# A decoder layer on one core: first batch's x^T in row-tile order, its 1/std in one pass, and a new order of the instructions

## Chip, cores and metric

The kernel runs on 1 core of a Trainium2 chip. The metric is device microseconds of one execution, lower is better. The kernel before takes 381.44 us (median of 3 runs, 380.48 to 382.34).

## The reference

Eight batches of 512 tokens with 256 features go through one decoder layer, all in float32:

```python
x = x + attn(layernorm(x), head_mask, w_q, w_k, w_v, w_o)   # one head of 128; softmax(q k^T / sqrt(128)) v
x = x + xattn(layernorm(x), ctx, mask, W, b)                # relu(x W^T + b) against relu(ctx W^T + b), masked softmax, times ctx
x = x + ffn(layernorm(x), w_gate, w_up, w_down)             # 256 -> 1024 -> 256, silu(gate) * up
```

In the ffn the activations are rounded to whole multiples of max|row|/127, and the weights to -1, 0 or 1 times the mean of |w|. Layer normalisation is (x - mean) / sqrt(var + 1e-5) over the features.

## The kernel before, in words

There are three streams per batch. Stream A is self-attention, B is cross-attention, C is the ffn. E prepares the context side of B (YP0 and YP1, relu(ctx W^T + b) by halves), W and F load and prepare the weights. Everything is written out by hand in five tables, one for each engine (`PE_ORDER`, `ACT_ORDER`, `DVE_ORDER`, `POOL_ORDER`, `SP_ORDER`). An entry such as `A.S0/3` is stream, step and batch, and each engine runs its table in order, with semaphore waits in front of each step. The three streams of different batches run through each other: A is one to two batches ahead of B, and B one ahead of C. The tables alone decide what stands behind what.

To keep float32 accuracy, each operand of a matmul in A, B and E is split into hi (rounded to fp32r, on ACT) and lo (the rest, on DVE or POOL), and a product is three matmuls (hi hi, hi lo, lo hi; L1047 to L1049). A 512-wide block is one PSUM bank. PE therefore carries most of the work. ACT copies PSUM to the hi part and does exp, relu, tanh and silu. DVE makes lo parts, row maxima, statistics (`bn_stats`, `bn_aggr`) and residual additions. POOL makes other lo parts (L617 to L630), 1/std (an addition and a power), gate times up (L674) and rounding. SP issues DMAs.

A takes the layer norm out of the matmul: the weights are centred, q, k and v are computed from the raw x^T (`a_xT_raw`, 2 chunks of 128 features by 512 tokens), and 1/std of each token is applied later: to the scores as a row vector over the keys (`r_bc`, 128 x 512, the same row on all partitions) and as a per-partition factor over the queries, and to v^T (`vT`, L1444).

Partition p of a tile of x holds tokens 4p to 4p+3 (own_tokens), so 1/std of a batch is a 128 x 4 tile `a_rstd`, and its columns are in the order (t p) where x^T has token order (p t). For batches 1 to 7 `r_bc` comes by a DMA through DRAM (`r_rows`). For batch 0 it is made on the core: `a_rstd` (128 x 4) is split into `r0_hi` (ACT, L814) and `r0_lo` (DVE, L1316), each is spread over a diagonal with `ident` (`spread_r0`, L1321, into `hT_hi` and `hT_lo`), and PE multiplies by ones (step W.r, L1269 and L1271, bank b0), so that each partition gets the row. ACT copies it to `r_bc` and turns (t p) into (p t) in its output pattern (`set_r0`, L818). q of any batch is written back from (p t) to (t p) by the copy that makes q_hi (L795) and q_lo (L1415), so that 128 consecutive columns are one tile of queries. The trace leaves digits out of names: `r_hi` and `r_lo` are `r0_hi` and `r0_lo`.

The first steps are: loads of the first context, of w_qkv, W and x; column sums of w_qkv on PE (L1262) and centring on DVE (`centre`, L1551, two instructions); YP0 and YP1 of batch 0; the split of w_qkv (ACT L980, then DVE `W.split`, L1556), which Q of batch 0 waits for; Q, K, V; W.r; then VT (transposes of v^T, L1082), the scores S0 to S3, exp, the transposes P0 to P3 (L1093), H and Y. YP1 of batch 0 uses bank b0, so W.r must wait until ACT has read it (L859, L860), and each relu on ACT waits for POOL to have taken the lo part of the one before (L625).

## Time and profile before

| | |
|---|---|
| median of 3 runs | 381.44 us (380.48 to 382.34) |
| the profiled execution, its own time | 382.19 us |
| its span | 380.2 us |
| TensorE busy (PE) | 364.1 us, 96% |
| DVE, ACT, POOL busy | 319.8 (84%), 320.0 (84%), 294.2 us (77%) |
| DMA | 36.92 MB, mean 97 GB/s |

The span is what the profiler saw between the first and the last instruction, and the execution's own time holds 2.0 us more around it. Busy time of PE counts an overlap of matmuls that follow each other, since one matmul is reported with a duration of 0.39 us although the next starts 0.23 us after it.

### The profile page before, as it was taken

The page shows a single profiled execution, that of the slowest core. Times are in us where ns is not written, and L with a number is a line of the kernel's source. Part 1 is how long each engine was busy: PE and PEld are TensorE (multiplying, and loading weights), DVE is VectorE, ACT ScalarE, POOL GpSimd, SP SyncE. Part 2 cuts the span into 40 slices and gives each one's busy share as a digit, 9 for nine tenths or more (in the row PEclk, how much of TensorE's full clock was granted, in tenths as well). Part 3 has the DMA queues.
Part 4 walks back from the last instruction along what each step waited for, and adds up shares of the span by engine and source line. Part 5 has one row for each costly group of instructions (what it writes and reads, how often), then busy time and mean ns, then how long its engine had stood idle before and what let it go on. Part 6 is the DMA issues. An engine that isn't in the chain of part 4 may idle for free.

```text
span 380.2 us, 7393 instructions
## 1 busy us (share of the span) xinstructions
PE 364.1 (96%) x2113; PEld 284.7 (75%) x2142; DVE 319.8 (84%) x921; ACT 320.0 (84%) x598; POOL 294.2 (77%) x425
## 2 busy tenths in 40 slices
...
PEclk9989999999999999999999999999999999999999
...
DMA packets 48167, 36.92 MB, mean 97 GB/s; under 512 B 39552, under 2 KB 41216, under 8 KB 47744
## 3 DMA queue, kind: packets, MB, share of 16 engines
...
## 4 chain that ended last, share of the span: by engine, by line
PE 79%; ACT 7%; DVE 5%; DMA 4%; issue 3%; POOL 1%; ACTq 0%; DVEq 0%; POOLq 0%; SPq 0%
PE b_bank L1047 9%; PE b_bank L1049 9%; PE b_bank L1048 9%; PE d_bank L1251 7%; PE a_bank L1047 6%; PE a_bank L1049 6%; PE a_bank L1048 6%; PE g_bank L1235 5%; PE u_bank L1235 5%; PE b_bank L1163 3%; PE a_bank L1093 3%; DMA a_xT_raw<-in_x_t 2%; PE e_bank L1047 1%; PE e_bank L1049 1%; PE e_bank L1048 1%
## 5 line engine op out<-in xcount | busy, mean ns | idle before, releaser
L674 POOL TENSOR_TENSOR c_work<-c_work 128x512 f32<-128x512 f32 x48 | 61.8, 1290 | 18.1 <-DVE c_work L1491 16.1
L716 POOL TENSOR_SCALAR c_work<-c_work,h_q 128x1024 f32<-128x1024 f32 x31 | 34.9, 1125 | 11.5 <-DVE h_q L1511 11.5
L1504 DVE TENSOR_REDUCE h_max<-c_work 128x1 f32<-128x1024 f32 x32 | 38.8, 1213 | 4.2 <-POOL c_work L674 3.6
L935 ACT ACTIVATE c_work<-g_bank,c_tanh_scale 128x512 f32<-128x512 f32 x52 | 36.0, 692 | 6.4 <-PE g_bank L1235 4.9
L1047 PE MATMUL b_bank<-ctx_hi,b_pT_hi 128*128 128x256 f32 x128 | 38.6, 302 | 0.0
L1491 DVE SCALAR_TENSOR_TENSOR c_work<-c_work,g_bank 128x512 f32<-128x512 f32 x52 | 35.3, 679 | 2.1 <-ACT c_work L935 1.8
L1049 PE MATMUL b_bank<-ctx_hi,b_pT_lo 128*128 128x256 f32 x128 | 36.1, 282 | 0.0
L1048 PE MATMUL b_bank<-ctx_lo,b_pT_hi 128*128 128x256 f32 x128 | 36.1, 282 | 0.0
L1251 PE MATMUL d_bank<-downT,c_half 128*128 128x256 bf16 x256 | 33.3, 273 | 1.5 <-ACT a_xT_raw L962 0.9
L945 ACT ACTIVATE c_half<-c_work 128x1024 bf16<-128x1024 f32 x28 | 29.7, 1066 | 4.1 <-POOL c_work L716 4.1
L1235 PE MATMUL g_bank<-gateT,xqT 128*128 128x512 bf16 x98 | 30.5, 381 | 1.5 <-ACT xqT L908 0.5
L1251 PEld LDWEIGHTS d_bank<-downT,c_half 128*128 128x128 bf16 x256 | 23.9, 98 | 10.3 <-issue 3.0
L1235 PE MATMUL u_bank<-upT,xqT 128*128 128x512 bf16 x97 | 30.3, 381 | 1.0
L938 ACT ACTIVATE c_work<-u_bank 128x512 f32<-128x512 f32 x48 | 29.0, 603 | 1.8 <-PE u_bank L1235 1.5
L625 POOL TENSOR_TENSOR yp_lo<-e_relu,yp_hi 128x512 fp32r<-128x512 f32 x16 | 20.7, 1293 | 9.7 <-ACT yp_hi L860 9.7
L1047 PE MATMUL b_bank<-yp_hi,xp_hi 128*128 128x512 f32 x64 | 28.0, 437 | 0.0
L847 ACT ACTIVATE b_pT_hi<-b_bank 128x512 fp32r<-128x512 f32 x32 | 19.2, 599 | 9.4 <-PE b_bank L1163 9.4
L1047 PEld LDWEIGHTS b_bank<-ctx_hi,b_pT_hi 128*128 128x128 f32 x128 | 24.3, 190 | 2.4 <-issue 0.7
L838 ACT ACTIVATE a_p<-a_p,a_nmax 128x512 f32<-128x512 f32 x32 | 23.5, 733 | 2.7 <-DVE a_nmax L1437 2.7
L869 ACT ACTIVATE b_p<-b_p,b_nmax 128x512 f32<-128x512 f32 x32 | 23.3, 731 | 2.3 <-DVE b_nmax L1469 2.3
L1049 PE MATMUL b_bank<-yp_hi,xp_lo 128*128 128x512 f32 x64 | 25.2, 393 | 0.0
L1048 PE MATMUL b_bank<-yp_lo,xp_hi 128*128 128x512 f32 x64 | 25.1, 392 | 0.0
...
## 6 DMA issues: line engine op xcount, KB each, us to landing
...
c_work<-in_w_up SPq DMA_DIRECT2D x1, 1024.0 KB, 10.2
```

The costliest lines, as they stand in the source:

```text
L674: pool.tensor_tensor(h[:, t % 2, half * HALF:(half + 1) * HALF], th[:, j % 2, :], up[:, j % 2, :], ALU.mult).then_inc(hs, 1)
L716: pool.tensor_scalar(h[:, t % 2, :], h[:, t % 2, :], h_q[:, t:t + 1], ROUND if n < LAST else ROUND_F16, ALU.mult, ALU.add).then_inc(h_roun ...
L935: act.activation(th[:, j % 2, :], gu_bank("g", j, n), ACT.Tanh, scale=c_tanh_scale[:, j // 2:j // 2 + 1]).then_inc(tanhs, 1)
L938: act.activation(up[:, j % 2, :], gu_bank("u", j, n), ACT.Copy).then_inc(ups, 1)
L945: act.activation(h_q8[:, t % 2, :], h[:, t % 2, :], ACT.Copy, bias=-ROUND).then_inc(hqs, 1)
L1047: pe.matmul(dst, l_hi, r_hi, start=first, stop=False)
L1048: pe.matmul(dst, l_hi, r_lo, start=False, stop=False)
L1049: return pe.matmul(dst, l_lo, r_hi, start=False, stop=last)
L1235: mm = pe.matmul(dst, xqT[:, t * DC + c, :], w[:, c, cols], start=c == 0, stop=c == DC - 1)
L1251: mm = pe.matmul(d_bank[:, 0:D], h_T[:, t % 2, f, :], downT[:, f, :], start=f == 0, stop=f == FC - 1)
L1491: dve.scalar_tensor_tensor(th[:, j % 2, :], th[:, j % 2, :], 1.0, gu_bank("g", j, n), ALU.add, ALU.mult).then_inc(gates, 1)
L1504: dve.tensor_reduce(h_max[:, one], h[:, t % 2, :], AX.X, ALU.max, apply_absolute_value=True).then_inc(h_maxes, 1)
```

## The change

1. The host lays x^T of batch 0 out as (t p), in row-tile order; batches 1 to 7 stay as they were. So `set_r0` copies the bank to `r_bc` straight, and q_hi and q_lo of batch 0 are straight copies too.
2. 1/std of batch 0 is one addition and one power over 128 x 4 (`a_rstd_first`) in place of two of each over 128 x 2. It starts when both halves of the statistics are there.
3. `r0_lo` is made by four instructions of one column each (tensor_scalar with the hi column as its scalar) in place of one over 128 x 4.
4. All five order tables are new. Among others: SP loads W ahead of the second half of the first context, and x of batch 1 ahead of the second half of x of batch 0; PE runs W.r ahead of V.

```diff
@@ PE_ORDER (one line of it shown)
-    W.colsum/0 E.YP0/0 E.YP1/0 A.Q/0 A.K/0 A.V/0 W.r/0 A.VT/0 A.S0/0 A.S1/0 A.S2/0 A.S3/0 A.P0/0 A.P1/0 A.Q/1
+    W.colsum/0 E.YP0/0 E.YP1/0 A.Q/0 A.K/0 W.r/0 A.V/0 A.VT/0 A.S0/0 A.S1/0 A.S2/0 A.S3/0 A.P0/0 A.P1/0 A.Q/1
...
@@ POOL_ORDER
-    A.rs0/0 A.rs1/0 E.YP0/0 A.rs0/1 A.rs1/1 E.YP1/0 A.xT0/1 A.xT1/1 E.ctxT/1 A.rs0/2 A.rs1/2 B.ctx/0 E.YP0/1
+    A.rs0/0 E.YP0/0 E.YP1/0 A.rs0/1 A.rs1/1 A.xT0/1 A.xT1/1 A.rs0/2 A.rs1/2 E.ctxT/1 A.xT0/2 A.xT1/2 B.ctx/0
...
@@ SP_ORDER
-    W.c0/0 W.qkv/0 W.c1/0 W.W/0 W.x0/0 W.x1/0 S.x/1 W.bias/0 W.o/0 W.hm/0 F.gate/0 F.up/0 F.down/0 S.ctx/0
+    W.c0/0 W.qkv/0 W.W/0 W.c1/0 W.x0/0 S.x/1 W.x1/0 W.bias/0 W.o/0 W.hm/0 F.gate/0 F.up/0 F.down/0 S.mask/0
...
+            def a_rstd_first():
+                pool.wait_ge(a_mvs, 2)
+                pool.tensor_tensor(a_var[:, :], a_mv[:, :, 1], eps[:, :], ALU.add).then_inc(a_rstds, 2)
+                pool.wait_ge(a_rstds, 2)
+                pool.tensor_tensor(a_rstd[:, 0, :], a_var[:, :], neg_half[:, :], ALU.pow).then_inc(a_rstds, 2)
             def a_rstd_part(half, n):
                 two = slice(2 * half, 2 * half + 2)
                 pool.wait_ge(a_mvs, 2 * n + half + 1)
-                if n > 0:
-                    pool.wait_ge(a_rstds, 4 * (n - 1) + 2 * half + 2)
+                pool.wait_ge(a_rstds, 4 if n == 1 else 4 * (n - 1) + 2 * half + 2)
...
-                    a_rstd_part(int(name[2]), n)
+                    a_rstd_part(int(name[2]), n) if n > 0 else a_rstd_first()
...
+                elif step == "Q" and n == 0:
+                    act.activation(q_hi[:, :], src[:, :], ACT.Copy, scale=SCALE).then_inc(a_his, 1)
...
             def set_r0():
                 act.wait_ge(r0_filled, 1)
-                act.activation(r_bc[:, :].rearrange("k (p t) -> k t p", t=T), b0_bank[:, :].rearrange("k (t p) -> k t p", t=T),
-                               ACT.Copy).then_inc(r0_set, 1)
+                act.activation(r_bc[:, :], b0_bank[:, :], ACT.Copy).then_inc(r0_set, 1)
...
             def split_r0_rest():
                 dve.wait_ge(r0_his, 1)
-                dve.tensor_tensor(r0_lo[:, :], a_rstd[:, 0, :], f32(r0_hi[:, :]), ALU.subtract).then_inc(r0_los, 1)
+                for t in range(T):
+                    last = dve.tensor_scalar(r0_lo[:, t:t + 1], a_rstd[:, 0, t:t + 1], f32(r0_hi[:, t:t + 1]), None, ALU.subtract)
+                last.then_inc(r0_los, 1)
...
-                    if step == "Q":
+                    if step == "Q" and n == 0:
+                        last = dve.scalar_tensor_tensor(q_lo[:, :], src[:, :], SCALE, f32(q_hi[:, :]), ALU.mult, ALU.subtract)
+                    elif step == "Q":
...
     x, ctx = inputs["x"], inputs["ctx_1024"]
+    x_t = x.reshape(*x.shape[:2], -1, P).transpose(3, 0, 2, 1).copy()
+    x_t[:, 0] = x_t[:, 0].reshape(P, x_t.shape[2], P, -1).swapaxes(2, 3).reshape(P, *x_t.shape[2:])
```

What the tables do is seen in the instructions of an engine in their order (line numbers are those of each kernel; code lines of the new one stand up to 12 further on).

DVE at the start, from the last split of the first inputs to the spread of 1/std. Before:

```order
L1326 TENSOR_TENSOR ctxT_lo<-ctxT_raw,ctxT_hi 128x512
L1568 TENSOR_TENSOR wt_lo<-xqT,wt_hi 128x512
L1551 SCALAR_TENSOR_TENSOR b_p<-b_bank,b_p 128x384 x2
L1304 BN_STATS a_bn<-x_all 128x6 x4
L1311 BN_AGGR a_mv<-a_bn 128x2 x2
L1556 TENSOR_TENSOR wqkv_lo<-b_p,wqkv_hi 128x768
L1311 BN_AGGR a_mv<-a_bn 128x2 x2
L1304 BN_STATS a_bn<-x_all 128x6 x4
L1311 BN_AGGR a_mv<-a_bn 128x2 x4
L1316 TENSOR_TENSOR r_lo<-a_rstd,r_hi 128x4
```

DVE in the changed kernel, the same place:

```order
L1334 TENSOR_TENSOR ctxT_lo<-ctxT_raw,ctxT_hi 128x512
L1310 BN_STATS a_bn<-x_all 128x6 x2
L1561 SCALAR_TENSOR_TENSOR b_p<-b_bank,b_p 128x384 x2
L1310 BN_STATS a_bn<-x_all 128x6 x2
L1317 BN_AGGR a_mv<-a_bn 128x2 x2
L1571 CAST hm_f<-hm_i 128x1
L1317 BN_AGGR a_mv<-a_bn 128x2 x2
L1310 BN_STATS a_bn<-x_all 128x6 x2
L1566 TENSOR_TENSOR wqkv_lo<-b_p,wqkv_hi 128x768
L1310 BN_STATS a_bn<-x_all 128x6 x2
L1574 SCALAR_TENSOR_TENSOR wo_lo<-b_p,hm_f,wo_hi 128x256
L1323 TENSOR_SCALAR r_lo<-a_rstd,r_hi 128x1 x4
```

`ctxT_lo` and `wt_lo` are the second context half and W; `b_p` is the centring of w_qkv and `wqkv_lo` its split, which Q waits for. The statistics of batch 0 (two of four `BN_STATS`) now come ahead of the centring, and two of batch 1's ahead of `wqkv_lo`; the scaling of w_o (`hm_f`, `wo_lo`), which stood behind `q_lo`, now comes ahead of `r_lo`.

ACT at the start, from YP0 of batch 0 to the copies of 1/std and k. Before:

```order
L859 ACTIVATE e_relu<-e_bank,bias 128x512
L860 ACTIVATE yp_hi<-e_bank,bias 128x512
L814 ACTIVATE r_hi<-a_rstd 128x4
L795 ACTIVATE q_hi<-a_bank 128x512
L830 ACTIVATE gateT,w_sum<-c_work 128x1024
L859 ACTIVATE e_relu<-b_bank,bias 128x512
L860 ACTIVATE yp_hi<-b_bank,bias 128x512
L830 ACTIVATE gateT,w_sum<-c_work 128x1024
L818 ACTIVATE r_bc<-b_bank 128x4x128
L798 ACTIVATE k_hi<-a_bank 128x512
```

ACT in the changed kernel, the same place:

```order
L865 ACTIVATE e_relu<-e_bank,bias 128x512
L866 ACTIVATE yp_hi<-e_bank,bias 128x512
L830 ACTIVATE wo_hi<-b_p,hm_f 128x256
L821 ACTIVATE r_hi<-a_rstd 128x4
L865 ACTIVATE e_relu<-b_bank,bias 128x512
L866 ACTIVATE yp_hi<-b_bank,bias 128x512
L799 ACTIVATE q_hi<-a_bank 128x512
L836 ACTIVATE gateT,w_sum<-c_work 128x1024
L805 ACTIVATE k_hi<-a_bank 128x512
L825 ACTIVATE r_bc<-b_bank 128x512
```

`e_bank` is YP0 and `b_bank` under L859/L865 is YP1; `gateT,w_sum` is a sum over half of an ffn weight. YP1 moved ahead of `q_hi` and of the first sum, `k_hi` ahead of `r_bc`, and the second sum behind both.

ACT near the end, from the last copy of B's output (`a_xT_raw<-b_bank`, O3 of batch 7) to the third rounded row tile of the ffn of batch 6 (`c_half`). Before:

```order
L953 ACTIVATE a_xT_raw<-b_bank,b_inv 128x256
L935 ACTIVATE c_work<-g_bank,c_tanh_scale 128x512
L908 ACTIVATE xqT<-e_bank 128x256
L935 ACTIVATE c_work<-a_bank,c_tanh_scale 128x512
L962 ACTIVATE a_xT_raw<-d_bank,h_out 128x256
L902 ACTIVATE c_xn<-c_xn,pos_round,c_q 128x256
L897 ACTIVATE c_xn<-x_all,c_shift,c_rstd 128x256
L923 ACT_TABLE_LOAD
L923 ACTIVATE c_work<-g_bank,c_tanh_scale 128x512
L908 ACTIVATE xqT<-e_bank 128x256
L945 ACTIVATE c_half<-c_work 128x1024
```

ACT in the changed kernel, between the same two ends:

```order
L959 ACTIVATE a_xT_raw<-b_bank,b_inv 128x256
L903 ACTIVATE c_xn<-x_all,c_shift,c_rstd 128x256
L929 ACT_TABLE_LOAD
L929 ACTIVATE c_work<-g_bank,c_tanh_scale 128x512
L903 ACTIVATE c_xn<-x_all,c_shift,c_rstd 128x256
L929 ACTIVATE c_work<-a_bank,c_tanh_scale 128x512
L908 ACTIVATE c_xn<-c_xn,pos_round,c_q 128x256
L951 ACTIVATE c_half<-c_work 128x1024
```

`ACT_TABLE_LOAD` and `c_work<-g_bank` under L923/L929 is the first silu of batch 7. Eleven rows became eight: two tanh of batch 6 (L935), two copies of `xqT` and one of the ffn output (L962) are no longer between the two ends, and a second silu and a second norm (L897/L903) are.

## Rows read from the trace of the kernel before

**Rows 1.** The page: TensorE's busy time, and its granted clock in 40 slices.
```profile
PE 364.1 (96%) x2113; PEld 284.7 (75%) x2142; DVE 319.8 (84%) x921; ACT 320.0 (84%) x598; POOL 294.2 (77%) x425
...
PEclk9989999999999999999999999999999999999999
```

**Rows 2.** Windows by stage: busy us of PE, PEld, DVE, ACT, POOL, PEclk, DMA, GB/s.
```profile
19.00:27.00 8.00, 5.96 (x23) 4.50 (x24) 5.50 (x16) 7.06 (x15) 3.35 (x3) 0.79 0.75 258
27.00:57.00 30.00, 28.23 (x153) 23.22 (x152) 23.40 (x82) 28.64 (x53) 24.72 (x22) 1.00 0.40 118
57.00:354.00 297.00, 294.71 (x1734) 232.55 (x1760) 258.79 (x750) 253.14 (x479) 240.21 (x344) 1.00 0.31 77
354.00:372.70 18.70, 15.90 (x113) 9.25 (x114) 17.69 (x42) 17.86 (x33) 15.52 (x34) 1.00 0.22 44
```

**Rows 3.** Timeline of the first 23 us: start us, us taken, engine, line, instruction.
```profile
9.52 1.02 DVE L1551 SCALAR_TENSOR_TENSOR b_p<-b_bank,b_p 128x384 f32<-128x384 f32 x2
...
9.66 0.50 PE L1047 MATMUL e_bank<-ctxT_hi,wt_hi 128*128 128x512 f32 x1 [0.44 <-DVE wt_lo L1568]
...
10.46 1.40 DVE L1304 BATCH_NORM_STATS2 a_bn<-x_all 128x6 f32<-128x256 f32 x4
...
11.91 0.93 DVE L1556 TENSOR_TENSOR wqkv_lo<-b_p,wqkv_hi 128x768 fp32r<-128x768 f32 x1
...
12.90 0.51 PE L1047 MATMUL a_bank<-a_xT_hi,wqkv_hi 128*128 128x512 f32 x1 [0.19 <-DVE wqkv_lo L1556]
...
13.92 0.70 POOL L653 TENSOR_TENSOR a_rstd<-a_var,neg_half 128x2 f32<-128x2 f32 x1
...
14.59 1.29 POOL L625 TENSOR_TENSOR yp_lo<-e_relu,yp_hi 128x512 fp32r<-128x512 f32 x1
...
14.89 1.00 DVE L1316 TENSOR_TENSOR r_lo<-a_rstd,r_hi 128x4 fp32r<-128x4 f32 x1
...
17.42 1.06 ACT L830 ACTIVATE gateT<-c_work 128x1024 f32<-128x1024 f32 x1
...
17.64 0.47 PE L1269 MATMUL b_bank<-hT_hi,ones_r 128*128 128x512 f32 x1 [0.38 <-issue]
...
18.46 1.09 ACT L818 ACTIVATE r_bc<-b_bank 128x512 f32<-128x512 f32 x1
...
19.32 0.65 ACT L798 ACTIVATE k_hi<-a_bank 128x512 fp32r<-128x512 f32 x1
...
20.40 0.66 PE L1082 MATMUL u_bank<-ident,vT 128*128 128x128 f32 x4 [2.05 <-DVE vT L1444]
...
22.49 0.63 PE L1048 MATMUL a_bank<-k_lo,q_hi 128*128 128x512 f32 x1
...
22.91 0.63 PE L1049 MATMUL a_bank<-k_hi,q_lo 128*128 128x512 f32 x1
```

**Rows 4.** Timeline of PE: the first matmuls of Q of batch 1.
```profile
27.06 0.47 PE L1047 MATMUL d_bank<-a_xT_hi,wqkv_hi 128*128 128x512 f32 x1
27.37 0.39 PE L1048 MATMUL d_bank<-a_xT_lo,wqkv_hi 128*128 128x512 f32 x1
27.60 0.40 PE L1049 MATMUL d_bank<-a_xT_hi,wqkv_lo 128*128 128x512 f32 x1
```

**Rows 5.** Windows of the start: the granted clock from 22 to 24 us.
```profile
22.00:24.00 2.00, 2.00 (x6) 1.55 (x5) 1.18 (x3) 1.96 (x5) 0.48 (x1) 0.50 0.96 376
```

**Rows 6.** Timeline of PE from 41 to 55 us: the two waits.
```profile
47.87 0.47 PE L1047 MATMUL e_bank<-ctxT_hi,wt_hi 128*128 128x512 f32 x1 [0.92 <-ACT yp_hi L860]
...
53.77 0.36 PE L1047 MATMUL a_bank<-wo_hi,hT_hi 128*128 128x256 f32 x1 [0.63 <-DVE hT_lo L1423]
```

**Rows 7.** Timeline of ACT near the end: O3 of batch 7, third tile of batch 6.
```profile
354.82 0.46 ACT L953 ACTIVATE a_xT_raw<-b_bank,b_inv 128x256 f32<-128x256 f32 x1
...
360.23 1.06 ACT L945 ACTIVATE c_half<-c_work 128x1024 bf16<-128x1024 f32 x1
```

**Rows 8.** Timeline of DVE near the end: first gate product of batch 7.
```profile
361.42 0.69 DVE L1486 TENSOR_TENSOR c_work<-c_work,u_bank 128x512 f32<-128x512 f32 x1 [0.16 <-ACT c_half L945]
```

280 lines of the change are left out of this document (140 added, 140 removed).

## The prediction

> **What bounds the kernel now.** I read four views, in this order. First the page: TensorE is busy 364.1 of 380.2 us, no other engine is over 84%, and its granted clock is full but for one dip in the third slice [rows 1]. Then the windows by stage, for where PE's idle time lies [rows 2]: 2.0 us from 19 to 27, 1.8 us from 27 to 57, only 2.3 us in the 297 us from 57 to 354, and 2.8 us from 354 to 372.7. In the long middle PE is the bound. All its matmuls are still there after the change, and so a new order of them can give back idle time, and nothing else: at most 1.8 + 2.3 = 4.1 us between 27 and 354, however good it is. Its two largest pieces are single waits of 0.92 us on ACT's relu (YP of the context side) and 0.63 us on DVE's lo part of h [rows 6]. The third view is the timeline of the first 27 us, where PE waits for other engines [rows 3, 4], and the last is the timeline near the end, where ACT and DVE pace the last ffn [rows 7, 8]. A microsecond gained before Q of batch 1 at 27.06 us is worth about one at the end, since PE runs nearly without a gap from there. I ask three things: when does Q of batch 1 start, does the middle keep its idle time, and does the tail get shorter.
>
> **The start now.** YP begins at 9.66 us and Q at 12.90, as soon as `wqkv_lo` (11.91 to 12.84) is there. 1/std is ready at 14.62 (13.92 + 0.70). The one-row product starts at 17.64, the copy to `r_bc` takes 1.09 us from 18.46, and the transposes of v^T start at 20.40 after 2.05 us of idle PE [rows 3]. By 22 us the clock is at half, 1.2 of its 2.4 GHz (0.50 from 22 to 24 us [rows 5]): two score matmuls stand 0.42 us apart (22.49, 22.91 [rows 3]) where they stand 0.23 apart at full clock (27.37, 27.60 [rows 4]). The mean clock of 0.79 over the 8 us from 19 to 27 [rows 2] bounds the cost of the dip: 8 x 0.21 = 1.7 us of PE work.
>
> **The parts of the change.**
>
> *Straight copy to r_bc.* It took 1.09 us [rows 3]. The nearest copy of 128x512 out of PSUM without a reordered pattern is `k_hi`, 0.65 us [rows 3]. Gain 0.44 us, on the path to VT. Straight copies of q gain between 0 and 0.44; no row has q straight, and I take 0: they're hidden, since K and v^T are what the scores wait for.
>
> *1/std in one pass.* Two operations in place of four on POOL. The power over two columns took 0.70 us; over four I bound it by 0.70 and 1.40 and take 1.0, in the middle. For the addition in front of it I allow 0.2, a guess. The new pair starts when both halves of the statistics are there, about 12.4 (below), and ends at 13.6 where the old ended at 14.62: 1.0 us sooner. I cost it at nothing, because 1/std is not late: the row product also needs YP1's relus (its bank), the lo part and the spreads. If those cover it no more, it is worth 1.0.
>
> *r_lo by columns.* The old one took 1.00 us for four elements a partition, from 14.89 to 15.89, and POOL's `yp_lo` ran from 14.59 to 15.88: it stood behind POOL [rows 3]. Four single columns cost from 4 x 0.07 to 1.29 us (the same stand behind POOL); I take 0.3. Gain 0.7, hidden by ACT, see below.
>
> *The new DVE order.* W comes before the second context half now, so one DVE instruction of 0.6 to 0.7 us (a 128x512 one took 0.69 [rows 8]) is no longer ahead of `wt_lo`: YP begins at 9.0, and its twelve matmuls of 0.23 end at 11.8. But half of the statistics (0.70 of 1.40 us [rows 3]) now stands ahead of the centring, and half of batch 1's (0.70) ahead of `wqkv_lo`. Counting on from 9.5: statistics to 10.2, centring to 11.15, the other statistics to 11.85, 0.45 for aggregates and a small cast to 12.3 (a guess), statistics of batch 1 to 13.0. So `wqkv_lo` starts 1.1 us later than now. There it meets POOL's power (12.6 to 13.6), and as `r_lo` shows, such a pair does not run together. I let it wait until 13.6. It ends at 14.4, and **Q starts at 14.4 in place of 12.90**, with PE idle 2.6 us from 11.8.
>
> *The new ACT order.* YP0's relus end at 13.2, the copies of w_o and r_hi at 13.9; YP1's relus must wait for POOL's lo part of YP0, which itself stands behind `wqkv_lo`: 14.4 to 15.7. So YP1 ends at 16.9, q_hi at 17.5, one ffn sum (1.06 us and 0.2 to read it out [rows 3]) at 18.7, k_hi at 19.3, r_bc at 19.9. The spreads on DVE, behind POOL's two lo parts, are ready between 17.2 and 18.9, so they are covered. v^T follows at 20.5, and VT starts at 20.6 in place of 20.40. The straight copy's 0.44 us and the rest are spent on the later split and on YP1, sum and k ahead of it.
>
> *The clock.* An idle PE of 2.05 us is followed by the half clock now; the new idle stretch of 2.6 us lies earlier, before Q and K. I expect the dip there, over the twelve matmuls of Q and K: K's copy and then V come later, VT at 21.6, but the scores run at full clock and end at about 25.0 (now 25.4). Counting exp and transposes behind them, Q of batch 1 starts at 27.1: no change. With the dip on the scores as now it is 27.3 (+0.2); without any dip 26.3 (-0.8). The Trainium skill, TensorE: Matmul & The Clock Gate, section "Why this matters for your kernels", lets the clock fall only for pauses longer than the 2.05 us seen here. The trace speaks against that: it fell. By the rule the start would come out at -0.8.
>
> **Start: 0.0 us** (from -0.8 to +1.5, the upper end below).
>
> *The middle.* Loads and stores move, and so do the lanes of all streams. **0.0 us**: the bound below is -4.1 (all idle time gone), the bound above I set at the same +4.1, and I take the zero between, since I see no reason why a new order should make more waits vanish than appear; the two single waits stay, since what stands ahead of them on ACT is exchanged for work of the same length (a sum or sign of 1.0 us against two relus).
>
> *The tail.* Between the copy of O3 (354.82) and the third rounded tile of batch 6 (360.23), ACT passes 5.4 us; that tile releases the first gate product of batch 7 at 361.42, which starts the row of products and maxima that DVE runs to the end [rows 7, 8]. Now eight operations and a table load stand between, then five and a table load: less by two tanh, two small copies and one of 128x256 out of PSUM, and more by a silu and a norm. Taking the load as 1.3 us, the copy and eight operations share 4.1 us, 0.46 each, and three of them are 1.4 us. Against it, O3 on PE comes behind four more gate and up steps (two matmuls of 0.23 each, 1.8 in sum) and no longer behind one down step (eight of half that width, 0.9): 0.9 us later. **-0.5 us**, between -1.4 (O3's lateness costs nothing) and +0.9 (ACT was not the limit).
>
> **Sum:** 0.0 + 0.0 - 0.5 = -0.5 us on the profiled execution's own 382.19 us, 381.7. That execution stands 0.75 us above the median of the three, so on the median: 381.44 - 0.5 = **380.9 us**.
>
> **The rivals.**
>
> *A, faster: the dip is gone and the order packs better.* The row product is ahead of V now, so V's 1.4 us of matmuls fill what was an idle PE; with PE fed, the clock stays up. Start -0.8, tail -0.5, and half of the 4.1 us of idle middle won, -2.0: 381.44 - 3.3 = 378.1. For it: the idle time is real, and the straight copy is on the path. Against: an idle stretch of 2.6 us arises before Q. The skill's rule on the clock, above, belongs here. Chance 0.33.
>
> *B, slower: `wqkv_lo` loses its turn to POOL.* If POOL takes `yp_lo` (1.29 us) straight after the power, `wqkv_lo` runs from 14.9 and Q starts at 15.7. Everything of batch 0 is then late by up to 1.3 us, and the clock dips on Q and again after the wait before VT. It decides once POOL gets the turn: +1.5 at the start, and +1.0 in the middle, where A's later batches then meet B's work, with the tail at -0.5: 381.44 + 2.0 = 383.4. For it: `r_lo` waited for the whole of a `yp_lo`. Against: DVE asks first here. Chance 0.22. Nearby, the middle alone could be 2 us worse.
>
> *C: the change does nothing at the start, and the tail neither,* because 1/std was not late and O3's lateness eats ACT's gain: 381.4, inside the forecast's band. Chance 0.12.
>
> My forecast has the remaining 0.33.
>
> **The numbers.** A measurement of this kernel can tell about 0.5%, 1.9 us. Faster than 379.5: most of A and a little of the forecast, 0.34. Slower than 383.3: half of B, 0.11, and 0.09 from the forecast and C where the middle comes out 2 us worse. Within: 0.46. The range goes from A, with 0.5 us more of the middle, 377.6, to B with 0.4 more, 383.8.
>
> **What would show each step.** Right: the row of `r_bc` takes 0.6 to 0.65 us; `r_lo` takes 0.1 to 0.2 for one column; `a_rstd` of batch 0 is one row of about 1.0 us before 14 us; YP begins near 9.0 and Q after 14.0, with over 2 us of idle PE between; the clock falls before 18 us; Q of batch 1 starts at 26.5 to 27.5; PE idles 3 to 5 us from 27 to 354; the first silu's gate product stands under 6.1 us behind the copy of O3 (now 6.6). Wrong: Q before 13.5 (DVE's order costs nothing), Q of batch 1 before 26 or after 28, or PE's idle time in the middle below 2 or above 6 us, which would move the time more than all of the start.

## The result and the profile after

The changed kernel takes **385.22 us** (median of 5 runs, 384.90 to 386.25) beside 381.44 us before (5 runs, 380.48 to 382.77): ratio 1.0099, 95% interval 1.0082 to 1.0116. It is 1% slower, 3.8 us, and outside the range of the prediction. The profiled execution took 384.94 us, with a span of 383.0 in place of 380.2.

The windows by stage (busy us of PE, PEld, DVE, ACT, POOL, then PEclk, DMA, GB/s), after:

```profile
19.00:27.00 8.00, 5.34 (x25) 4.24 (x26) 5.86 (x23) 7.41 (x18) 3.39 (x5) 0.89 0.92 298
27.00:57.00 30.00, 28.15 (x149) 23.28 (x148) 21.12 (x70) 26.74 (x48) 24.25 (x21) 0.97 0.42 117
57.00:354.00 297.00, 293.47 (x1719) 231.94 (x1743) 256.68 (x747) 255.27 (x478) 239.31 (x340) 1.00 0.34 75
354.00:372.70 18.70, 16.48 (x104) 10.04 (x106) 16.58 (x40) 16.43 (x30) 14.95 (x36) 0.91 0.30 72
```

Against [rows 2]: PE leaves 3.5 of the 297 us from 57 to 354 idle (297.00 - 293.47), where it left 2.3. Both figures are too high by much the same: these two traces hold 2115 and 2113 matmuls for 2142 weight loads, and in this stretch 24 and 26 matmuls have no row (before's lacks gate and up matmuls, 195 rows for 224). What they took counts as idle time. The profiles with all 2142 and the old order behind the start leave 0.3 to 0.6 us idle there (e1, e3 and e14 below). Its clock is 0.89 from 19 to 27 us (0.79 before), but 0.97 behind that and 0.91 in the tail, where it was full.

The timeline of the first 28 us, after (start us, us taken, engine, line, instruction, idle time before it and what ended it):

```profile
8.48 0.50 PE L1053 MATMUL e_bank<-ctxT_hi,wt_hi 128*128 128x512 f32 x1 [0.66 <-DVE wt_lo L1578]
...
12.21 1.03 POOL L646 TENSOR_TENSOR a_rstd<-a_var,neg_half 128x4 f32<-128x4 f32 x1
12.27 0.94 DVE L1566 TENSOR_TENSOR wqkv_lo<-b_p,wqkv_hi 128x768 fp32r<-128x768 f32 x1
...
13.27 0.50 PE L1053 MATMUL a_bank<-a_xT_hi,wqkv_hi 128*128 128x512 f32 x1 [1.74 <-DVE wqkv_lo L1566]
...
17.75 0.61 ACT L825 ACTIVATE r_bc<-b_bank 128x512 f32<-128x512 f32 x1
...
19.26 0.66 PE L1088 MATMUL u_bank<-ident,vT 128*128 128x128 f32 x4 [0.86 <-DVE vT L1454]
...
19.67 0.48 PE L1053 MATMUL d_bank<-k_hi,q_hi 128*128 128x512 f32 x1
...
19.91 0.63 ACT L882 ACTIVATE mask_add<-mask_u 128x512 f32<-128x512 uint8 x1 [0.50 <-DMA mask_u<-in_mask]
...
21.48 0.58 ACT L805 ACTIVATE v_hi<-u_bank 128x512 fp32r<-128x512 f32 x1
...
23.00 0.62 ACT L813 ACTIVATE a_xT_hi<-a_xT_raw 128x512 fp32r<-128x512 f32 x1
...
23.52 0.71 ACT L844 ACTIVATE a_p<-a_p,a_nmax 128x512 f32<-128x512 f32 x1
23.69 2.51 POOL L617 TENSOR_TENSOR a_xT_lo<-a_xT_raw,a_xT_hi 128x512 fp32r<-128x512 f32 x2 [4.20 <-ACT a_xT_hi L813]
...
24.23 0.61 ACT L813 ACTIVATE a_xT_hi<-a_xT_raw 128x512 fp32r<-128x512 f32 x1
...
24.47 0.63 PE L1099 MATMUL g_bank<-ident,a_p 128*128 128x128 f32 x4 [1.80 <-ACT a_p L844]
...
26.43 0.78 PE L1053 MATMUL d_bank<-a_xT_hi,wqkv_hi 128*128 128x512 f32 x1
```

The first score matmul and the first exp of before, for comparison:

```profile
21.00 0.50 PE L1047 MATMUL d_bank<-k_hi,q_hi 128*128 128x512 f32 x1
...
24.44 0.72 ACT L838 ACTIVATE a_p<-a_p,a_nmax 128x512 f32<-128x512 f32 x1 [0.48 <-DVE a_nmax L1437]
```

This answers to [rows 3]. YP starts at 8.48 (9.66 before), Q at 13.27 (12.90), the copy to r_bc takes 0.61 us (1.09) and stands at 17.75 (18.46), VT at 19.26 (20.40), and the first scores at 19.67 (21.00), 1.3 us sooner and at full clock. So far the change does more than I forecast. Then it is given back. ScalarE (ACT) waits 0.50 us for the first mask's load, and a sum, v_hi and another sum follow, then x^T of batch 1 at 23.00 and the first exp at 23.52: 0.9 us sooner than before (24.44), of the 1.3. PE has stood idle for 1.80 us when the first exp's transposes begin. The other half of x^T stands behind that exp, at 24.23, POOL's lo parts of both halves end at 26.20 (23.69 + 2.51), and Q of batch 1 starts at 26.43: 0.6 us sooner [rows 4]. And it starts at half clock: its first matmul takes 0.78 us, where that of Q took 0.50.

In the middle, the waits of PE from 57 to 354 us (waiter, releaser: us in total, times, longest us), in before and after:

```profile
PE a_bank L1093 <- ACT a_p L838: 0.3, 1, 0.3
```

```profile
PE d_bank L1257 <- DMA c_half<-c_half: 0.6, 1, 0.6
PE a_bank L1088 <- DVE vT L1454: 0.4, 2, 0.2
PE g_bank L1241 <- issue: 0.2, 1, 0.2
PE g_bank L1241 <- DVE c_work L1501: 0.2, 1, 0.2
PE b_bank L1053 <- POOL xp_lo L630: 0.2, 1, 0.2
```

Before has one such wait, and that is all the view lists: 0.3 us. After, the waits come to 1.6 us, and the largest is PE's wait for a transposing DMA of the ffn's activations, which ends at 120.80 us, ahead of the first down step of batch 0. The tail, after, in the timeline of ACT and DVE, and the window of 2 us in which its clock is lowest:

```profile
357.09 0.47 ACT L959 ACTIVATE a_xT_raw<-b_bank,b_inv 128x256 f32<-128x256 f32 x1 [1.00 <-PE b_bank L1055]
...
361.50 1.05 ACT L951 ACTIVATE c_half<-c_work 128x1024 bf16<-128x1024 f32 x1
...
362.68 0.69 DVE L1496 TENSOR_TENSOR c_work<-c_work,u_bank 128x512 f32<-128x512 f32 x1 [0.73 <-ACT c_half L951]
...
363.10 0.53 PE L1241 MATMUL g_bank<-gateT,xqT 128*128 128x512 bf16 x1 [1.16 <-ACT xqT L914]
```

```profile
364.00:366.00 2.00, 2.00 (x10) 0.96 (x8) 1.90 (x3) 1.79 (x4) 1.03 (x4) 0.50 0.63 118
```

The first gate product of batch 7 stands 5.6 us behind the copy of O3 (357.09 to 362.68), where it stood 6.6 us behind [rows 7, 8]. But PE then idles 1.16 us ahead of a gate step at 363.10, and its clock is at 0.50 from 364 to 366 us.

### The profile page after: what moved, and what is told of

Read it like the earlier page. It is cut to its first block, busy times and chain, and to the rows that moved or that the text cites. A ratio compares the mean times of both kernels' runs of the same rounds, so it can differ in the third digit from the quotient of the medians.

```text
span 383.0 us, 7397 instructions
## 1 busy us (share of the span) xinstructions
PE 364.0 (95%) x2115; PEld 285.2 (74%) x2142; DVE 318.4 (83%) x924; ACT 322.2 (84%) x598; POOL 293.0 (76%) x423
## 4 chain that ended last, share of the span: by engine, by line
PE 60%; POOL 14%; ACT 7%; DMA 6%; issue 6%; DVE 4%; SPq 2%; ACTq 0%; POOLq 0%; DVEq 0%
PE b_bank L1053 7%; PE b_bank L1055 7%; PE b_bank L1054 7%; PE d_bank L1257 5%; PE a_bank L1053 4%; PE g_bank L1241 4%; PE a_bank L1055 4%; PE a_bank L1054 4%; POOL c_work L679 4%; PE u_bank L1241 4%; DMA mask_u<-in_mask 3%; PE b_bank L1169 3%; PE a_bank L1099 2%; POOL xp_lo L630 1%; PE a_bank L1241 1%
## 5 line engine op out<-in xcount | busy, mean ns | idle before, releaser
L1241 PE MATMUL u_bank<-upT,xqT 128*128 128x512 bf16 x100 | 31.4, 386 | 0.8
L617 POOL TENSOR_TENSOR a_xT_lo<-a_xT_raw,a_xT_hi 128x512 fp32r<-128x512 f32 x14 | 17.9, 1287 | 9.8 <-ACT a_xT_hi L813 9.8
L1054 PEld LDWEIGHTS b_bank<-ctx_lo,b_pT_hi 128*128 128x128 f32 x128 | 24.4, 191 | 0.4
```

The lines of the kernel that those rows point to most:

```text
L1054: pe.matmul(dst, l_hi, r_lo, start=False, stop=False)
L1241: mm = pe.matmul(dst, xqT[:, t * DC + c, :], w[:, c, cols], start=c == 0, stop=c == DC - 1)
```

## The experiments

The theory to begin with: the order costs the time, and most of it behind the start, where the profiled pair shows PE's idle time grow. Its rivals: the edits cost it, or the start does. Before stands at 381.3 to 382.1 us in the five sets of runs, so ratios to it are what to compare. A ratio of 0.0026 is 1 us.

**The edits or the order?** Two kernels: the local edits in the order of before, and the new order with the instructions of before.

```diff
 e1: every ORDER table as before, the rest as in the change
-    A.rs0/0 A.rs1/0 E.YP0/0 A.rs0/1 A.rs1/1 E.YP1/0
+    A.rs0/0 E.YP0/0 A.rs0/1 A.rs1/1 E.YP1/0
 e2: the new tables, the rest as before
-    A.rs0/0 E.YP0/0 E.YP1/0 A.rs0/1 A.rs1/1
+    A.rs0/0 A.rs1/0 E.YP0/0 E.YP1/0 A.rs0/1 A.rs1/1
```

> The local edits alone (row-tile order of x^T of batch 0, straight copies, 1/std in one pass, lo part by columns), with the five order tables of before. Theory (the new order costs the time, the edits save a little): 380.9 to 381.5, that is 0 to 0.5 us below before, the copy to r_bc 0.61 us in place of 1.09, and scores 0.4 us sooner. Rival (the edits cost: the addition and the power wait for both halves of the statistics, or four column instructions stand behind POOL): 382 to 384, with the one-row product later than the 17.6 us of before.

> The new order tables alone, with the instructions of before (reordering copy to r_bc, 1/std in two passes, lo part in one). Theory (order costs the time): 385 to 386, about as slow as the change or 0.5 us slower. Rival (edits cost): 381 to 383.

Measured: e1 381.79 us, ratio 1.0005 (0.9990 to 1.0020); e2 385.06 us, 1.0086 (1.0064 to 1.0108). The order costs the time, as the theory has it, and the edits give nothing that can be told (0.4 us less to 0.8 more). In e1's profile the path to the scores is shorter all the same:

```profile
17.97 0.59 ACT L820 ACTIVATE r_bc<-b_bank 128x512 f32<-128x512 f32 x1
...
20.02 0.50 PE L1048 MATMUL d_bank<-k_hi,q_hi 128*128 128x512 f32 x1
...
25.27 0.47 PE L1048 MATMUL d_bank<-a_xT_hi,wqkv_hi 128*128 128x512 f32 x1
```

The copy takes 0.59 us, the first score stands 1.0 us sooner than before, and Q of batch 1 at 25.27 in place of 27.06, with a clock of 1.00 in every window up to 372.7 us. But this was the fastest of twelve executions (380.37), and the median shows nothing of those 1.8 us. Of before's 23 executions in this set, 14 have a mean granted clock of at least 0.998, with a median of 381.0, and 9 a lower one, with 381.8. The dip is worth 0.8 us, and it comes and goes.

**Which part of the order?** The tables are cut where both orders have issued the same steps: PE behind B.XP0/0, ACT behind B.norm1/0, DVE behind A.Y1/1, POOL behind B.rs1/0, SP behind S.rb/1. PE comes to its cut some 53 to 57 us into the program, and SP, whose queue runs ahead, at some 36 us.

```diff
 e3: the change, and in every table behind the cut the order of before, PE:
     A.Y0/1 A.Y1/1 B.XP0/0
-    A.Q/2 B.XP1/0 A.K/2 E.YP0/3 A.V/2 B.S0/0
+    B.XP1/0 A.Q/2 A.K/2 E.YP0/3 A.V/2 B.S0/0
 e4: the reverse, before the cut the order of before, PE:
-    A.K/0 W.r/0 A.V/0 A.VT/0
+    A.K/0 A.V/0 W.r/0 A.VT/0
```

> The change's instructions; the new order up to B.XP0 of batch 0 on TensorE (and the same place on the other engines), the order of before behind it. Theory 1 (the loss sits where the profiled pair shows it grow: start +0.2, middle +1.5, tail +1.0): 381.2 to 382.0, no slower than before. Rival (the later start of the sums, mask and exps in the first batch, and the half clock that moves to 25 to 29 us, set off the rest): 383.5 to 385.

> The change's instructions; the order of before up to B.XP0 of batch 0, the new order behind it. Theory 1 (the loss sits in the middle and the tail): 383.5 to 385, 2.5 to 3.5 us above before. Rival (the loss comes from the start): 380.5 to 382.

Measured: e3 383.22 us, 1.0037 (1.0020 to 1.0053); e4 388.77 us, 1.0176 (1.0149 to 1.0203). e3 lies between both theories: the new start costs 1.2 us against e1 by the ratios (1.4 by the medians) even with the old rest, though the two intervals just touch, so my reading of the profiled pair, +0.2, was wrong. e4 has a wait of its own at the cut:

```profile
35.21 0.67 ACT L874 ACTIVATE mask_add<-mask_u 128x512 f32<-128x512 uint8 x1
...
35.95 0.33 SPq L514 DMA_DIRECT2D mask_u<-in_mask  x1
...
36.37 0.38 SPq L486 DMA_DIRECT2D a_xT_raw<-in_x_t  x1
...
41.28 0.63 ACT L805 ACTIVATE a_xT_hi<-a_xT_raw 128x512 fp32r<-128x512 f32 x1 [4.70 <-DMA a_xT_raw<-in_x_t]
```

SP's queue runs in order too. The new order loads the third mask ahead of x^T of batch 2, and has the first mask's conversion (mask_add), which frees the buffer, early on ACT. With the old start that conversion ends at 35.88, the mask's load starts at 35.95, x^T behind it at 36.37, and ACT stands for 4.70 us. e5 mends only this:

```diff
 e5: as e4, SP_ORDER
-    S.rb/1 S.mask/2 S.xT/2 S.rw/2 S.ctxT/2 S.xT/3 S.ctx/1
+    S.rb/1 S.xT/2 S.ctxT/2 S.rw/2 S.mask/2 S.ctx/1 S.xT/3
```

> As the kernel with the new order behind the first 53 us only, but SP's queue keeps the order of before for ten entries more, so that x^T of batch 2 is issued ahead of the third mask. Theory (the 5 us stall at 38 us in the first version was the third mask's load standing in front of x^T of batch 2, and the rest of the new order costs 2 us, as the change against the kernel with the new start alone: 385.2 against 383.2): 383.5 to 384.5. Rival (the new rest needs the new start and costs more behind the old one): 386 to 388.

Measured: 382.58 us, 1.0011 (0.9998 to 1.0023). Below the range of the theory: the new rest costs 0.2 us against e1 here, and e5 is at most 0.9 us above before by its interval, while the change has the new rest 2.4 us above e3. Then the last piece alone:

```diff
 e6: the change, and behind B.S0/7 (PE), B.exp0/7 (ACT) and their like the order of before, PE:
-    B.S0/7 B.S1/7 C.g2/6 C.u2/6 C.g3/6 B.P0/7
+    B.S0/7 C.g2/6 B.S1/7 C.u2/6 B.P0/7 C.g3/6
```

> The change, with the order of before from the scores of the last batch's stream B (about 336 us) to the end. Theory (the tail of the new order costs 1.0 us, the stretch from 57 to 354 us 1.5): 384.0 to 384.5. Rival (lateness in the middle is lost anyway, the tail is no worse): 385.0 to 385.5. A third way: all 2.0 us of the rest lie in the tail: 383.0 to 383.4.

Measured: 385.74 us, 1.0087 (1.0071 to 1.0103). Before stood at 382.11 us in this set, so it's the ratio that counts, and it lies between the theory (1.0068 to 1.0081) and the rival (1.0094 to 1.0107), taken as ratios to 381.4. Against the change the tail's order costs 0.5 us, and with both intervals anything from 0.4 us of gain to 1.4 of cost fits. Most of the time goes ahead of it: e6 and e3 have the same start and the same tail, and e6 stands 1.9 us above e3, with intervals that do not touch. In their profiles the way from Q of batch 1 to the copy of O3 of batch 7 takes 330.5 us (28.49 to 359.03) and 328.8 us (27.12 to 355.88).

**What in the start?** In the start of the change three things looked suspect: the mask on ACT, the place of `wqkv_lo` on DVE, and x^T of batch 1 behind sums and exps.

```diff
 e7: the change, ACT_ORDER
-    F.sum1/0 B.mask/0 F.sum2/0 A.VT/0 F.sum3/0 A.xT0/1
+    F.sum1/0 F.sum2/0 A.VT/0 F.sum3/0 B.mask/0 A.xT0/1
 e9: the change, DVE_ORDER
-    A.ag0/0 W.wo0/0 A.ag1/0 A.bn0/1 W.split/0 A.bn1/1
+    A.ag0/0 W.split/0 A.ag1/0 W.wo0/0 A.bn0/1 A.bn1/1
 e10: both
```

> The change, with one entry of ScalarE's order moved: the first mask's conversion, which waits 0.50 us for its load at 19.9 us and stands ahead of two ffn sums and v_hi, goes two sums later. Theory (ScalarE's head-of-line wait makes v_hi and the exps late, and so part of the 1.4 us of the new start): 0.4 to 0.8 us below the change, 384.4 to 384.8, exp of tile 0 by 23.1 in place of 23.5. Rival (the exps wait for TensorE or the clock): no change, 385.0 to 385.5.

> The change, with two entries of VectorE's order moved: the split of w_qkv (wqkv_lo) stands right behind the first aggregates, ahead of the cast of the head mask (which waits 0.5 us for its load) and of half the statistics of batch 1. Theory (in the new order wqkv_lo starts about 1.2 us late and at the same moment as POOL's power, which then takes 1.85 us in place of 1.03 in the profiles of three kernels with this start): Q 1.0 to 1.3 us sooner, power 1.03, and 1.0 to 2.0 us below the change, 383.2 to 384.2 on a chip where before takes 381.4 (ratio to before 1.005 to 1.007). Rival (1/std and the row product decide, Q's start is hidden): no change, 1.009 to 1.010.

> The one before, and in addition the first mask's conversion on ScalarE two ffn sums later, which alone gave 0.4%. Theory (two separate head-of-line waits of the new start, which add): ratio to before 1.001 to 1.004. Rival (both buy the same microsecond): the same as the better of the two alone, 1.0055 to 1.0065.

Measured: e7 384.84 us, 1.0057 (1.0036 to 1.0078); e9 385.02 us, 1.0100 (1.0075 to 1.0124); e10 384.72 us, 1.0095 (1.0074 to 1.0116). e7 is 1.6 us better than the change by its ratio, twice what the theory gave at most. But e10, with the same edit, is no better than the change and misses both of its ranges (1.001 to 1.004, and 1.0055 to 1.0065), so the mask's place isn't shown to matter. e9 decides for its rival. Its profile against that of e3, which has the same start but for that edit (DVE `wqkv_lo`, POOL power and lo part of YP0, ACT relu of YP1), first e3:

```profile
12.71 1.85 POOL L640 TENSOR_TENSOR a_rstd<-a_var,neg_half 128x4 f32<-128x4 f32 x1
12.74 0.94 DVE L1560 TENSOR_TENSOR wqkv_lo<-b_p,wqkv_hi 128x768 fp32r<-128x768 f32 x1
...
14.54 1.33 POOL L619 TENSOR_TENSOR yp_lo<-e_relu,yp_hi 128x512 fp32r<-128x512 f32 x1
...
15.99 0.69 ACT L859 ACTIVATE e_relu<-b_bank,bias 128x512 f32<-128x512 f32 x1 [1.19 <-POOL yp_lo L619]
```

and e9:

```profile
11.75 0.96 DVE L1558 TENSOR_TENSOR wqkv_lo<-b_p,wqkv_hi 128x768 fp32r<-128x768 f32 x1
...
13.39 1.03 POOL L638 TENSOR_TENSOR a_rstd<-a_var,neg_half 128x4 f32<-128x4 f32 x1
...
14.38 1.37 POOL L617 TENSOR_TENSOR yp_lo<-e_relu,yp_hi 128x512 fp32r<-128x512 f32 x1
...
15.87 0.69 ACT L857 ACTIVATE e_relu<-b_bank,bias 128x512 f32<-128x512 f32 x1 [1.22 <-POOL yp_lo L617]
```

In e3 the power, begun 0.03 us ahead of `wqkv_lo`, takes 1.85 us, 0.82 more than alone. In e9 they are apart, `wqkv_lo` is 1.0 us sooner and the power takes 1.03, but it starts later, as its aggregates stand behind the split: it ends at 14.42 in place of 14.56. The relu of YP1, which waits for POOL's lo part behind that power, stands at 15.87 in place of 15.99. So 1/std and YP1's relu set the pace there, and not Q. The change's own profile bears this out: its power ends at 13.24, 1.3 us ahead of that of e3, and its scores start at 19.67 in place of 21.05.

**ACT's order.** e13 puts the split of x^T together and a sum behind the exps; e14 puts ACT's new start alone into the order of before (with W and w_o early, e8 below), and e16 takes it out of the change alone.

```diff
 e13: the change, ACT_ORDER
-    F.sum2/0 A.VT/0 F.sum3/0 A.xT0/1 A.exp0/0 A.xT1/1 A.exp1/0 A.P0/0 A.exp2/0 A.P1/0 E.ctxT/1 A.exp3/0 F.sum4/0
+    F.sum2/0 A.VT/0 A.xT0/1 A.xT1/1 A.exp0/0 A.exp1/0 A.P0/0 A.exp2/0 A.P1/0 E.ctxT/1 A.exp3/0 F.sum3/0 F.sum4/0
 e14: as e8, the first 42 entries of ACT_ORDER
-    W.rh/0 A.Q/0 F.sum0/0 E.YP1/0 F.sum1/0 W.r/0 A.K/0 F.sum2/0 F.sum3/0 A.VT/0 A.xT0/1 A.xT1/1 A.exp0/0
+    W.rh/0 E.YP1/0 A.Q/0 F.sum0/0 A.K/0 W.r/0 F.sum1/0 B.mask/0 F.sum2/0 A.VT/0 F.sum3/0 A.xT0/1 A.exp0/0
 e16: the change, with the - line of e14 in place of its + line, and SP_ORDER as in e5
```

> The change, with two entries of ScalarE's order moved: the second half of batch 1's x^T is split right behind the first (in the change an exp stands between), and the fourth ffn sum goes behind the last exp. Theory (ScalarE's order of the first 28 us is what the new start costs: in it x^T of batch 1 stands behind a sum and an exp, so exp of tile 0 comes 0.6 us late and POOL's lo part, which Q of batch 1 waits for, up to 1.2 us late): ratio to before 1.003 to 1.006, Q of batch 1 within 4.3 us of v_hi (4.95 us in the profile of the change, 3.9 in the one with the local edits alone). Rival (the loss is made behind 57 us, by waits that the start does not set): 1.0085 to 1.0105.

> The order of before with W first (ratio 0.996), but ScalarE's first 42 entries in the new order, the other four engines unchanged. Theory (ScalarE's order is the cost of the new start): 1.000 to 1.004, Q of batch 1 1.0 to 2.0 us later. Rival (the other engines' new orders at the start cost the time): 0.9955 to 0.9975.

> The change, with ScalarE's first 42 entries as in the order of before with W first, and SP's entries 23 to 30 as before (since the mask's conversion, which frees a buffer that SP waits for, is late again). Theory: most of the loss goes, ratio 0.999 to 1.004. Rival (VectorE's and SP's new order cost as much): 1.005 to 1.009.

Measured: e13 385.26 us, 1.0082 (1.0051 to 1.0114), unclear against the change, and its runs lie far apart (383.0 to 387.1). e14 383.86 us, 1.0057 (1.0039 to 1.0076): 2.6 us above the same kernel with the old ACT order if its second measurement is taken (e17, 0.9989), 3.7 us by its first (e8, 0.9960), and 3.1 us in the spans of the profiled pair (381.4 and 378.3). It lies above the theory's range (1.000 to 1.004) and far from the rival's. e16 389.05 us, 1.0179 (1.0158 to 1.0200). The timeline of e14 shows what ACT's order does when nothing else is changed:

```profile
15.71 0.69 ACT L859 ACTIVATE e_relu<-b_bank,bias 128x512 f32<-128x512 f32 x1 [1.14 <-POOL yp_lo L619]
...
18.86 0.61 ACT L819 ACTIVATE r_bc<-b_bank 128x512 f32<-128x512 f32 x1
...
20.92 0.50 PE L1047 MATMUL d_bank<-k_hi,q_hi 128*128 128x512 f32 x1
...
23.87 0.61 ACT L807 ACTIVATE a_xT_hi<-a_xT_raw 128x512 fp32r<-128x512 f32 x1
...
25.09 0.62 ACT L807 ACTIVATE a_xT_hi<-a_xT_raw 128x512 fp32r<-128x512 f32 x1
...
27.22 0.47 PE L1047 MATMUL d_bank<-a_xT_hi,wqkv_hi 128*128 128x512 f32 x1
```

ACT stands idle 1.14 us for POOL's lo part ahead of YP1's relu, with q_hi and a sum queued behind it. So r_bc is copied at 18.86, and the scores start at 20.92; in e8's profile it is 18.32 and 20.37. Then mask, sums and exps follow one another, x^T is split at 23.87 and 25.09, and Q of batch 1 starts at 27.22 in place of 25.63. In the windows of the same profile the clock is 0.79 from 19 to 27 us. e16 is inconclusive for its own question, since it has a wait like that of e4:

```profile
38.75 0.62 ACT L805 ACTIVATE a_xT_hi<-a_xT_raw 128x512 fp32r<-128x512 f32 x1
...
39.44 2.54 POOL L609 TENSOR_TENSOR a_xT_lo<-a_xT_raw,a_xT_hi 128x512 fp32r<-128x512 f32 x2 [6.74 <-ACT a_xT_hi L805]
```

POOL's new order takes x^T of batch 2 ahead of the first context's lo part, and ACT's old order splits it late: POOL stands for 6.7 us. The tables fit each other in pairs, and one of them can't be exchanged alone. That holds for e14 too: it shows what ACT's new start costs beside four old tables, and not what it costs in the change.

**Versions that might beat both.** e8 keeps the order of before, and takes from the new start that W comes first and w_o is split early; e12 moves sums on ACT in it, e11 takes DVE's new start.

```diff
 e8: as e1, SP_ORDER, ACT_ORDER, DVE_ORDER
-    W.c0/0 W.qkv/0 W.c1/0 W.W/0 W.x0/0
+    W.c0/0 W.qkv/0 W.W/0 W.c1/0 W.x0/0
-    W.cT1/0 W.hi/0 W.qkv/0 E.YP0/0 W.rh/0
+    W.hi/0 W.cT1/0 W.qkv/0 E.YP0/0 W.wo/0 W.rh/0
-    W.cT1/0 W.lo/0 W.centre/0 A.bn0/0 A.bn1/0 A.ag0/0 W.split/0 A.ag1/0
+    W.lo/0 W.cT1/0 W.centre/0 A.bn0/0 A.bn1/0 A.ag0/0 W.split/0 W.wo0/0 A.ag1/0
 e11: as e8, DVE_ORDER
+    W.lo/0 W.cT1/0 A.bn0/0 W.centre/0 A.bn1/0 A.ag0/0 W.wo0/0 A.ag1/0 A.bn0/1 W.split/0 A.bn1/1
 e12: as e8, ACT_ORDER
-    A.Q/0 F.sum0/0 E.YP1/0 F.sum1/0 W.r/0 A.K/0 F.sum2/0 F.sum3/0 A.VT/0 A.xT0/1
+    A.Q/0 E.YP1/0 A.K/0 W.r/0 F.sum0/0 F.sum1/0 A.VT/0 A.xT0/1
     (F.sum2/0 goes behind A.P1/0, F.sum3/0 behind A.exp3/0)
 e12, DVE_ORDER
-    A.Q/0 A.V/0 A.K/0
+    A.Q/0 A.K/0 A.V/0
```

> The change's instructions in the order of before, with only what I take to be the good of the new start: W is loaded, and split on ScalarE and VectorE, ahead of the second context half, and w_o is split at 12.4 us in place of 20. Theory (W's earlier place brings YP 0.7 to 1.1 us forward, and the cost of the new start came from its order of the statistics, sums and mask): 380.3 to 381.2, below the 381.79 of the local edits alone. Rival (wqkv_lo, which bounds Q, stays where it is, so that nothing is gained, or the longer idle stretch ahead of Q brings the clock down): 381.6 to 382.6.

> The suspected cost added to a good kernel: the order of before with W first (ratio 0.996), but VectorE's first twenty entries in the new order, so that wqkv_lo stands behind the cast and half the statistics of batch 1. Theory: Q 0.8 to 1.3 us later, the power stretched in part of the executions, ratio 0.9985 to 1.001. Rival (VectorE's order is hidden there): 0.995 to 0.997.

> The order of before with W first, and on ScalarE the relus of YP1, k_hi and the copy to r_bc ahead of the ffn sums, the copies of v and the next x^T ahead of two more of them. A try at a kernel faster than both. If ScalarE's order bounds the scores: scores 0.4 to 0.8 us sooner and ratio 0.994 to 0.9955. If the sums are only paid later, in the 30 us behind, where ScalarE is busy 28.6 of 30 us: 0.996 as without, or above.

Measured: e8 380.81 us, 0.9960 (0.9946 to 0.9974); e11 381.46 us, 1.0001 (0.9985 to 1.0017); e12 382.85 us, 1.0042 (1.0025 to 1.0059). e11 falls into its theory's range, 1.6 us above e8. But against the second measurement of the same kernel (e17 below, 0.9989) it is 0.5 us, which the intervals can't tell from nothing, so a cost of DVE's new start isn't shown. e12 asked for x^T of batch 1 before it was there:

```profile
22.88 1.15 ACT L808 ACTIVATE a_xT_hi<-a_xT_raw 128x512 fp32r<-128x512 f32 x2 [1.60 <-DMA a_xT_raw<-in_x_t]
...
24.88 0.63 PE L1094 MATMUL g_bank<-ident,a_p 128*128 128x128 f32 x4 [2.10 <-ACT a_p L839]
```

Two sums earlier, ACT finds x^T not loaded and stands 1.60 us; the sums are paid later, PE waits 2.10 us for the first exp, and its clock goes to 0.96 and 0.95 in the two windows from 19 to 57 us. Where ACT was seen to wait for this load, it came at 22.4 to 23.7 us (e12, e13, e15, e16), and in e1 it was there by 21.88. So ahead of x^T a sum can be free, and a load sets the earliest time of what is queued behind it. e8's gain was tried again, and with w_o's move alone:

```diff
 e17: e8, word for word
 e18: as e1, ACT_ORDER, DVE_ORDER
-    E.YP0/0 W.rh/0 A.Q/0
+    E.YP0/0 W.wo/0 W.rh/0 A.Q/0
-    W.split/0 A.ag1/0
+    W.split/0 W.wo0/0 A.ag1/0
```

> The kernel with W first and w_o split early once more, word for word, beside another set of runs of before. If its gain of 0.4% is real: ratio 0.9945 to 0.9975. If it was luck of six runs without a clock dip: 0.998 to 1.001, with dips in some of the runs.

> The local edits with the order of before, and only w_o's split moved from 20 us to ScalarE's wait for 1/std at 12.4 us; W stays behind the second context half. Theory (the exps of batch 0 are paced by ScalarE, so 0.5 us less ahead of them is the gain, and W's place gave none, since Q did not start sooner in the profiled pair): 0.9955 to 0.998. Rival (W's earlier place, which shortens the idle stretch ahead of the first products, is what kept the clock up): 0.9995 to 1.001.

Measured: e17 381.16 us, 0.9989 (0.9979 to 1.0000); e18 381.28 us, 0.9988 (0.9975 to 1.0000). The 0.4% of e8 did not come back: those six runs had no dip of the clock (before had one in 15 of its 17), while 4 of e17's 12 had one. What is left is 0.1%, 0.4 us, at the edge of what can be told. No kernel here is clearly faster than before.

**Start and rest together.** The last one asks what the new rest costs behind the best start.

```diff
 e15: e8 up to the cut of e4, the new order behind it, SP_ORDER as in e5
```

> The order of before with W first up to B.XP0 of batch 0, the new order behind it (with SP's ten entries more). Theory (the rest of the new order costs 0.3 to 1.2 us whatever the start: +0.0006 in the ratio against the local edits alone, +1.2 us in the profiled pair): 0.9965 to 0.9995. Rival (the new rest is as good as the old one if batch 0 is early): 0.9955 to 0.9965.

Measured: 382.44 us, 1.0014 (0.9998 to 1.0030), above both ranges. In its profile PE waits in the middle as after the change does, here from 57 to 354 us:

```profile
PE d_bank L1249 <- DMA c_half<-c_half: 1.1, 1, 1.1
PE g_bank L1233 <- DVE c_work L1493: 0.6, 2, 0.4
```

The four corners, as ratios to before:

| | old rest | new rest |
|---|---|---|
| old start | 1.0005 (e1) | 1.0011 (e5) |
| W first | 0.9960, 0.9989 (e8, e17) | 1.0014 (e15) |
| new start | 1.0037 (e3) | 1.0099 (the change) |

Taking the difference in a row at 3.8 us for 0.01: behind the old start the new rest costs 0.2 us, behind W first 1.0 to 2.1, behind the new start 2.4 us. The 2.2 us between the first row and the last are clear of noise: the four intervals taken together give 1.2 us either way. But e5 and e15 keep SP's order of before for ten entries behind the cut and the change doesn't, and no run gives the change with that order alone. So a part of those 2.2 us can be SP's.

The waits of PE from 57 to 354 us, as the same view lists them in all twenty profiles, go with the rest and not with the start:

| rest | profiles | PE's waits, sum | of them for the transposing DMA |
|---|---|---|---|
| old | before, e1, e3, e8, e11, e12, e14, e17, e18 | 0 to 0.3 us | none |
| new | e5, e10, e13 | 0.6 to 1.4 us | none |
| new | the change, e2, e4, e6, e7, e9, e15, e16 | 1.6 to 2.6 us | 0.6 to 1.3 us, once in each |

## Why the prediction was wrong, point by point

- **Straight copy to r_bc.** 0.44 us forecast, 1.09 to 0.61 us measured. Right, and worth nothing that the median can tell (e1), as is all that the edits do.
- **1/std in one pass.** I took 1.0 us for four columns, and 1.03 was measured. Right where it runs alone. I let `wqkv_lo` wait for it; it is the other way round. `wqkv_lo` takes 0.94 us each time, and the power 1.85 us where both begin together (e3, e6, e7, e11, e16).
- **r_lo by columns.** 0.3 us forecast, 0.56 to 0.58 measured for four, 0.14 a column. No row shows the 0.07 of my lower bound. Hidden, as forecast.
- **DVE's order.** YP at 9.0 forecast, 8.48 in the profile, and 9.6 in that of e6 with the same start. Q at 14.4 forecast, 13.27 measured (13.6 to 14.9 in e2, e3, e6 and e7), with PE idle 1.74 us ahead of it and not 2.6. The change's profile is below the 13.5 that I had named as a sign of being wrong; the other four are not. That Q would be the bound was wrong: Q came 1.0 us sooner in e9 and nothing followed.
- **ACT's order, the second step that failed.** I followed ACT to v^T and the scores ("the scores run at full clock and end at about 25.0"), and closed with "Counting exp and transposes behind them, Q of batch 1 starts at 27.1", by the distances of before. The scores began at 19.67, and Q of batch 1 only at 26.43: what stands between them on ACT and POOL, the mask, two sums, v_hi, and the halves of x^T with an exp between, was not counted at all. That 26.43 is ahead of the 27.06 of before is no gain, since the profile of before has the dip and not the edits. With the edits, Q of batch 1 starts at 25.3 to 26.2 behind the old start (e1, e5, e4) and at 26.4 to 28.5 behind the new one (the change, e13, e9, e3, e10, e7, e6). So "no change" should have been a loss of about 1 us, as the +1.2 of e3 against e1 has it. ACT's new start costs 2.6 us or more beside four old tables (e14); what it costs beside the new ones is not shown.
- **The clock.** The dip I expected before 18 us did not come in the profile of the change (PEclk 1.00 in its first 19 us). It came in that of e7, where the clock is 0.50 from 16 to 18 us, behind 1.94 us of idle PE ahead of Q. In the change it came behind 1.80 us of idle at 24.5, and in the tail behind 1.16 us. The Trainium skill (TensorE: Matmul & The Clock Gate, section "Why this matters for your kernels") warns only of idle gaps of TensorE that are longer than any of these. The traces do not agree: the clock fell behind each of them. It stayed full behind 1.57 us in e1 and 1.97 us in e11, so the length of the gap alone doesn't settle it. But the dips are a part only: of the five runs of the change, the one with a mean granted clock of 1.000 took 385.22, the median.
- **Start.** 0.0 forecast, from -0.8 to +1.5; +1.2 by the ratios of e3 and e1. Inside its bounds.
- **Middle. This is the step that failed.** The term was put at 0.0, between -4.1 and +4.1, on "I see no reason why a new order should make more waits vanish than appear". It measured +1.9 us by the ratios (e6 against e3, which differ in the middle alone), half of the 3.8. What stands there in its place are waits that were not there before: 1.6 us in the change's profile for 0.3, for a DMA transpose, and for POOL, DVE and v^T by 0.2 to 0.4 us. The order of before leaves PE waiting 0.3 us for one exp in 297 us; such an order can only get worse. The 2.3 us of idle time, from which I took a gain of up to 4.1 with the stretch before, were mostly matmuls without a row. The +1.0 that I gave rival B was the better value, and still too small. From 27 to 354 us PE idles 5.4 us by its busy time, outside the "3 to 5 us" of the signs for being right and inside the 6 of being wrong.
- **Tail.** -0.5 forecast. Right up to the first gate product, 5.6 us behind the copy of O3 where I had written "under 6.1 us". The half clock behind it took the gain back, and by e6 the new tail costs 0.5 us behind this middle, which can't be told from nothing. Edits 0.2, start 1.2, middle 1.9 and tail 0.5 make the 3.8.
- **Rivals.** B had the sign and, but for 1.8 us, the time (383.4), and not the mechanism: POOL never took the turn from `wqkv_lo`. A had nothing. The bound of 4.1 us of gain in the middle was of no use, and too wide; I should have asked how much could be lost.

What stays open: why the new start and the new rest cost more together (3.8 us) than apart (1.2 and 0.2), and how much of that is SP's ten entries. The waits for the transpose go with the new rest, in eight of its eleven profiles and in none of nine with the old one, but what makes it late is not shown, nor why it is missing in e5, e10 and e13. And e10, whose profile lists no such wait (it has 2115 of 2142 matmuls), is as slow as the change (1.0095), so that wait alone is hardly the cost.
